# Dealing buffers, PSUM halves and two loads anew in the start of a two-layer conditioned convolution kernel

## The chip, the cores and the metric

The kernel runs on one core of a Trainium2 chip. TensorE multiplies into PSUM (eight banks, here two halves A and B of four banks each), VectorE (DVE) and ScalarE (ACT) read PSUM and SBUF, GpSimd (POOL) works in SBUF, and SyncE (SP) issues transfers. ScalarE issues a few transfers too; SP's and ScalarE's transfers go by two queues through the same 16 DMA engines. Everything is float32. The metric is device time in microseconds (us).

## The reference

128 samples `x[b]` of 128 channels by 2048 positions pass four residual layers, whose parameters depend on a vector `cond[b]` of 128 numbers:

```python
x = x + conv1d(x, w0, groups=4, taps=9, pad=4) + (cond @ c0.T)[:, :, None] + bias
x = x + einsum('boi,bih->boh', agg_w1, x) + agg_b1[:, :, None]
x = x + conv1d(x, w2, groups=4, taps=9, pad=4) + (cond @ c2.T)[:, :, None] + bias
x = x + einsum('boi,bih->boh', agg_w3, x) + agg_b3[:, :, None]
```

with, for layers 1 and 3, `att = softmax(mlp(cond))` over 8 experts, `agg_w = einsum('bk,koi->boi', att, weight)` (one 128 x 128 matrix for each sample) and `agg_b = att @ bias_k`.

## The kernel before, in words

**Two parts.** A start of some 65 us computes everything that depends on `cond` and is the same for all positions. Then a pipeline over 64 pairs of samples does the four layers. The trip of the pipeline for pair i is a step; steps 0 and 1 and the last four are written out, the others are a hardware loop.

**The start.** TensorE computes the attention and the bias table, then the *matrix sets*: for each of the two mixing layers the 128 matrices of 128 x 128 are computed in 8 sets of 2048 columns (16 sets in all, numbered j = 0 to 15, the first eight for the first mixing layer). A set is one `aggregate`: matmuls that fill one half of PSUM (L347), from `rows`, the experts' weights. It is then *evicted*, that is, copied from PSUM to a buffer in SBUF, its *home*: by ScalarE (`take_agg`, L576) or VectorE (L738, for the sets in `BY_DVE`). Then SP stores it to DRAM (`mix_dram`, `store_agg`, L227), 1 MB each. The homes are buffers that the pipeline uses later: `shared[0..1]` and `y[0..1]`. `AHEAD` = 14 sets are made before the first convolution, the last two between it and the first mix. Semaphores: `taken(j)` says that set j was evicted (TensorE may reuse the half), `agg_stored[j]` that its store has landed (its home may be reused). `half_of(j)` is the PSUM half and `home_of[j]` the home.

**Beside it.** SP loads the taps of the two convolutions (`load_taps(v)`, 0.75 MB each) and the inputs of the pairs (`load_x_on`, 2 MB a pair). GpSimd works the taps over (L289 to L294), first those of layer 0, then those of layer 2. VectorE makes four *differences* of a pair's inputs (BOTH, SIGNED, ONLY_EVEN, ONLY_ODD; `diff_of_xin`, L695), which the convolution's matmuls read instead of the inputs; four more of the first two layers' output (`diff_of_x2`) feed the second convolution.

**A convolution** (`conv`, L373) is 224 matmuls. ScalarE copies the sums out in six parts (`take_sums`, L603 to L616): three into `shared`, three into `y`. The third of five parts of the matmuls (ONLY_EVEN) waits for the first copy and for all four differences. VectorE then makes the two halves of the output in `y` (L748, L750). **A mix** (`mix`, L441) is 128 matmuls of `y` with the pair's matrices, which `load_mix_on` loads from `mix_dram` into `mixw` (L167, four transfers); ScalarE evicts it (L664, L625).

The order of step 0 on TensorE is: convolution of pair 0, sets 14 and 15, first mix of pair 0; then comes the convolution of pair 1, and then the second convolution of pair 0. Each engine works its instructions in the order written; the kernel has no scheduler. The waits that matter are these lines:

```python
        BY_DVE = (2, 4)
...
                if j >= len(homes):
                    act.wait_ge(agg_stored[same_home_before(j)], 16)
...
                    conv(0, 0, taken(AHEAD - 1), taken(AHEAD - 2), (1, 2, 4), nothing)
...
                    mix(0, 0, taken(AHEAD), taken(AHEAD), taken(AHEAD + 1), nothing)
```

The first two arguments of `conv` and `mix` after the numbers are the semaphores for the halves: the first convolution begins in half A.

## Time and profile before

| what | us |
|---|---|
| median of three runs (2497.75 to 2498.95) | 2497.8 |
| the profiled execution | 2493.67 |
| its span, from the first to the last instruction | 2491.9 |
| TensorE matmuls busy in it | 2460.8 (99%) |
| VectorE busy | 2136.1 (86%) |
| ScalarE busy | 1523.4 (61%) |
| GpSimd busy | 32.0 (1%) |

The times of the trace count from the start of the span of the profiled execution. A busy TensorE need not be TensorE at its peak. The DMA engines are busy 90% or more in the first fortieth of the span and about 40% in the others.

### The profile page before, as it was taken

Reading aid. Unit: us, or ns where it says so; the run is one execution under the profiler, and the core shown is the slowest. Engines: PE = TensorE matmul, PEld = TensorE weight load, DVE = VectorE, ACT = ScalarE, POOL = GpSimd, SP = SyncE. Lnnn points to the kernel's source line nnn. Section 1 sums busy time; section 2 is a strip of 40 time slices with the busy share of each in tenths; the row PEclk is TensorE's granted clock in tenths of the full one; section 3 lists DMA queues with packets and bytes.
Section 4 is the critical chain, followed back from the end, with each engine's and each line's share of the span. In section 5 each row is a group of like instructions: output and inputs, shape, how many; then the busy total and the mean of one; then the engine's idle time right before and its main releaser. Section 6 shows DMA issues by size and latency. Waiting matters only on the chain.

```text
span 2491.9 us, 99092 instructions
## 1 busy us (share of the span) xinstructions
PE 2460.8 (99%) x45256; PEld 1402.0 (56%) x45256; DVE 2136.1 (86%) x796; ACT 1523.4 (61%) x1116; POOL 32.0 (1%) x28
## 2 busy tenths in 40 slices
PE   7999999999999999999999999999999999999998
PEld 3444444444555555555666666666666666666664
DVE  6988988889889889889889888898898898898883
ACT  5566666666666666666666666666666666666665
POOL 5000000000000000000000000000000000000000
PEclk9999999999999999999999999999999999999999
DMA  9444444444444444444444454444444444444433
GB/s 361 149 145 150 126 132 159 130 126 157 138 126 145 149 126 137 152 132 126 150 145 126 137 157 128 127 159 135 126 150 144 126 142 150 129 128 154 139 95 120
DMA packets 186682, 357.23 MB, mean 143 GB/s; under 512 B 12754, under 2 KB 143834, under 8 KB 154010
## 3 DMA queue, kind: packets, MB, share of 16 engines
q1 hardware_dynamic: 184824, 352.50, 45.2%
q10 hardware_dynamic: 1826, 4.23, 0.5%
q8 instruction: 29, 0.48, 0.1%
q14 instruction: 3, 0.02, 0.0%
HBM read 205.69 MB, written 150.99 MB: 143 GB/s over the span
## 4 chain that ended last, share of the span: by engine, by line
PE 97%; DMA 1%; ACT 1%; DVE 1%; issue 0%; SPq 0%; ACTq 0%
PE psum L373 61%; PE psum L441 35%; DMA mix_dram<-y 1%; DMA out<-outb 0%; ACT y L576 0%; DVE h L730 0%; PE psum L300 0%; ACT outb L625 0%; DVE y L727 0%; PE psum L347 0%; DVE diff L695 0%; DVE shared L738 0%; DVE y L738 0%; DVE y L750 0%; ACT y L612 0%
## 5 line engine op out<-in xcount | busy, mean ns | idle before, releaser
L373 PE MATMUL psum<-diff,prod_w 32*64 32x512 f32 x28672 | 1684.0, 588 | 8.0 <-ACT y L576 2.5
L373 PEld LDWEIGHTS psum<-diff,prod_w 32*64 32x64 f32 x28672 | 908.1, 131 | 684.4 <-issue 401.9
L695 DVE TENSOR_TENSOR diff<-xin 128x2052 f32<-128x2052 f32 x256 | 994.0, 3929 | 288.4 <-PE psum L373 288.4
L441 PE MATMUL psum<-y,mixw 32*64 32x512 f32 x16384 | 1020.1, 588 | 5.5 <-ACT y L576 3.4
L441 PEld LDWEIGHTS psum<-y,mixw 32*64 32x64 f32 x16384 | 545.8, 131 | 371.2 <-issue 221.1
L695 DVE TENSOR_TENSOR diff<-x 128x2055 f32<-128x2055 f32 x256 | 571.2, 2299 | 4.7 <-ACT x L664 4.7
L625 ACT ACTIVATE outb<-psum,bias_now 128x2048 f32<-128x2048 f32 x129 | 252.2, 1956 | 197.9 <-PE psum L441 196.3
L664 ACT ACTIVATE x<-psum,bias_now 128x2048 f32<-128x2048 f32 x128 | 252.8, 1975 | 195.4 <-PE psum L441 195.4
L603 ACT COPY shared<-psum 128x2048 f32<-128x2048 f32 x128 | 239.1, 1868 | 170.4 <-PE psum L373 169.5
L748 DVE TENSOR_TENSOR y<-y,shared 128x2048 f32<-128x2048 f32 x128 | 293.1, 2290 | 38.2 <-ACT y L614 38.2
L616 ACT COPY y<-psum 128x2048 f32<-128x2048 f32 x128 | 239.2, 1869 | 93.6 <-PE psum L373 93.6
L750 DVE TENSOR_TENSOR y<-y,shared 128x2048 f32<-128x2048 f32 x128 | 293.3, 2291 | 1.6 <-ACT y L616 1.5
L612 ACT COPY y<-psum 128x1024 f32<-128x1024 f32 x128 | 129.6, 1012 | 190.1 <-PE psum L373 190.1
L606 ACT COPY shared<-psum 128x1024 f32<-128x1024 f32 x128 | 129.6, 1013 | 80.6 <-PE psum L373 80.6
L608 ACT COPY shared<-psum 128x1024 f32<-128x1024 f32 x128 | 129.6, 1012 | 1.1 <-PE psum L373 1.0
L614 ACT COPY y<-psum 128x1024 f32<-128x1024 f32 x128 | 129.6, 1013 | 0.7 <-PE psum L373 0.6
L637 ACT COPY bias_now<-bias_table 128x12 f32 (+1 forms) x66 | 13.3, 201 | 15.3 <-issue 7.8
L576 ACT COPY shared<-psum 128x2048 f32<-128x2048 f32 x7 | 12.9, 1869 | 9.5 <-PE psum L347 9.5
L576 ACT COPY y<-psum 128x2048 f32<-128x2048 f32 x7 | 12.9, 1874 | 6.1 <-DMA mix_dram<-y 3.6
L347 PE MATMUL psum<-outb,att_t 32*128 32x512 f32 x64 | 10.4, 741 | 4.4 <-ACT y L576 1.8
L347 PE MATMUL psum<-diff,att_t 32*128 32x512 f32 x64 | 8.3, 619 | 3.6 <-DVE y L738 1.6
L347 PEld LDWEIGHTS psum<-outb,att_t 32*128 32x128 f32 x64 | 2.9, 209 | 12.0 <-ACT shared L576 6.0
(61 smaller groups left out, 83.3 us busy)
## 6 DMA issues: line engine op xcount, KB each, us to landing
out<-outb SPq DMA_DIRECT2D x127, 1024.0 KB, 4.8
xin<-x SPq DMA_DIRECT2D x126, 1024.0 KB, 6.8
mixw<-mix_dram SPq DMA_DIRECT2D x508, 128.0 KB, 5.5
mix_dram<-shared SPq DMA_DIRECT2D x8, 1024.0 KB, 12.5
mix_dram<-y SPq DMA_DIRECT2D x8, 1024.0 KB, 12.0
xin<-x ACTq DMA_DIRECT2D x2, 1024.0 KB, 10.9
y<-experts ACTq DMA_DIRECT2D x2, 512.0 KB, 4.6
prod_w<-conv_w SPq DMA_DIRECT2D x4, 256.0 KB, 7.9
```

What stands on the lines that cost most here:

```text
L373: return pe.matmul(psum[cols, half, g, :], prod_w[v][at, kind, s, cols], moving, start=start, stop=stop, skip_group_check=True)
L441: mm = pe.matmul(psum[cols, half, r, :], mixw[home][at, b, g, cols], y[home][at, :, g, b, :], start=g == 0, stop=g == GROUPS - 1)
L603: nc.scalar.copy(shared[v][:, 0], psum[:, A, :, :]).then_inc(shared_ready[v], 1)
L606: nc.scalar.copy(shared[v][:, 1, 0:2], psum[:, B_HALF, 0:2, :]).then_inc(shared_ready[v], 1)
L608: nc.scalar.copy(shared[v][:, 1, 2:4], psum[:, B_HALF, 2:4, :]).then_inc(shared_ready[v], 1)
L612: nc.scalar.copy(into[:, 0, 0:2], psum[:, A, 0:2, :]).then_inc(sums_taken[v], 1)
L616: nc.scalar.copy(into[:, 1], psum[:, B_HALF, :, :]).then_inc(sums_taken[v], 1)
L625: nc.scalar.activation(outb[:, b, :].rearrange("p (m j r) -> p m j r", j=PAR, r=PH)[:, at], psum[:, b, :, :].rearrange("p r (j m) -> p m j ...
L664: nc.scalar.activation(into, psum[:, b, :, :].rearrange("p r (j m) -> p j r m", j=PAR), ACT.Identity, bias=bias_now[:, 2 * PB + b, 0:1]).t ...
L695: nc.vector.tensor_tensor(into(kind), in0, in1, op).then_inc(diff_ready[v], 1)
L748: nc.vector.tensor_tensor(flat[:, 0], flat[:, 0], kept[:, 1], ALU.subtract).then_inc(y_ready[v], 1)
L750: nc.vector.tensor_tensor(flat[:, 1], flat[:, 1], kept[:, 0], ALU.add).then_inc(y_ready[v], 1)
```

## The change

It is confined to the start and to step 0.

- **Evictions.** VectorE evicts sets 3 and 5 (the fourth and the sixth) instead of 2 and 4. Set 2 goes to half A, and from there even sets go to A and odd ones to B; the first convolution starts in A behind set 12, and needs set 13's half later.
- **Homes.** There are ten instead of eight: both halves of `rows[0]` (which is `diff2`, free once the first eight sets are made) come in. Sets 14 and 15 go there and no longer to `y[1]`. VectorE's first `diff_of_x2`, which writes `diff2`, waits for their stores.
- **Loads.** The taps of layer 2 are loaded behind the first eight stores instead of before all. The inputs of pair 1 are issued by SP behind store 8, waiting there for the four differences of pair 0, instead of by ScalarE.
- **ScalarE.** The loads of pair 0's matrices (`first_matrices`) are issued behind the third copy of the first convolution instead of before the first. The first copy waits for store 6, the second for store 7, where the first waited for stores 8 and 9.
- **GpSimd.** Its work on the taps of layer 2 waits for the four differences of pair 0.

```diff
-        homes = [shared[0][:, 0], shared[0][:, 1], shared[1][:, 0], shared[1][:, 1],
-                 staging[:, 0], staging[:, 1], early[:, 0:2].rearrange("p n c -> p (n c)"),
-                 early[:, 2:4].rearrange("p n c -> p (n c)")]
+        homes = [shared[1][:, 0], shared[1][:, 1], early[:, 0:2].rearrange("p n c -> p (n c)"),
+                 early[:, 2:4].rearrange("p n c -> p (n c)"), staging[:, 0], staging[:, 1],
+                 shared[0][:, 0], shared[0][:, 1], rows[0][:, 0:PH * BANK], rows[0][:, PH * BANK:]]
...
-        home_of = [j % len(homes) for j in range(AHEAD)] + [4, 5]
-        LAST_IN_SHARED, LAST_IN_Y = ((8, 9), (10, 11)), ((6, 7), (14, 15))
+        home_of = list(range(len(homes))) + [0, 1, 4, 5, 8, 9]
+        LAST_IN_SHARED, LAST_IN_Y, LAST_IN_DIFF = ((6, 7), (10, 11)), ((2, 3), (12, 13)), (14, 15)
...
-            return A if j < 2 else 1 - j % 2 if j < AHEAD else j % 2
-
-        BY_DVE = (2, 4)
+            return A if j == 1 else j % 2
+
+        BY_DVE = (3, 5)
...
             load_rows(1)
-            load_taps(1)
...
-            for j in range(AHEAD):
+            for j in range(SETS):
                 store_agg(j)
+            load_taps(1)
+            store_agg(SETS)
+            sp.wait_ge(diff_ready[0], PRODUCTS)
+            load_x_on(sp, 1)
+            for j in range(SETS + 1, AHEAD):
+                store_agg(j)
...
+                if v == 1:
+                    pool.wait_ge(diff_ready[0], PRODUCTS)
...
+            pe.wait_ge(*taken(1))
+            aggregate(0, 2, half_of(2))
             pe.wait_ge(bias_ready, 2)
-            aggregate(0, 2, half_of(2))
-            for j in range(3, AHEAD):
+            aggregate(0, 3, half_of(3))
+            for j in range(4, AHEAD):
...
-                    conv(0, 0, taken(AHEAD - 1), taken(AHEAD - 2), (1, 2, 4), nothing)
+                    conv(0, 0, taken(AHEAD - 2), taken(AHEAD - 1), (1, 2, 4), nothing)
...
-                if j == AHEAD - 1:
-                    act.wait_ge(diff_ready[0], PRODUCTS)
-                    load_x_on(act, 1)
-
-            act.wait_ge(taps_ready, 1)
-            for j in range(SETS):
-                act.wait_ge(agg_stored[j], 16)
-            load_mix_on(act, 0, 0)
+
+            def first_matrices():
+                act.wait_ge(taps_ready, 1)
+                for j in range(SETS):
+                    act.wait_ge(agg_stored[j], 16)
+                load_mix_on(act, 0, 0)
...
-                    all_stored(LAST_IN_SHARED[v])
+                    act.wait_ge(agg_stored[LAST_IN_SHARED[v][0]], 16)
...
+                if whole(n) and n == 0:
+                    act.wait_ge(agg_stored[LAST_IN_SHARED[v][1]], 16)
...
+                behind_signed()
                 if whole(n) and n == 0:
-                    all_stored(LAST_IN_Y[v])
+                    for j in LAST_IN_Y[v]:
+                        act.wait_ge(agg_stored[j], 16)
...
+                if whole(i) and i == 0:
+                    take_sums(0, 0, behind_signed=first_matrices)
...
+                if whole(n) and n == 0:
+                    for j in LAST_IN_DIFF:
+                        dve.wait_ge(agg_stored[j], 16)
```

What this does to the order on ScalarE and on SP is seen best in the rows themselves. First ScalarE, from its tenth eviction of a set to the last copy of the first convolution, before the change (buffers by number; `mixw0` are the matrices of the first mixing layer, and a wait on `agg_stored9` is for the landing of set 9's store):

```order
L576 COPY y1<-psum 128x2048 [waits agg_stored4,agg_pe]
L576 COPY y1<-psum 128x2048 [waits agg_stored5,agg_pe]
L161 DMA xin<-x 128x2048 [waits diff_ready0]
L161 DMA xin<-x 128x2048
L167 DMA mixw0<-mix_dram0 32x8x128 [waits agg_stored4,agg_stored3,agg_stored5,agg_stored2,agg_stored6,agg_stored1,agg_stored7,agg_stored0,taps_ready]
L167 DMA mixw0<-mix_dram0 32x8x128 x3
L637 COPY bias_now<-bias_table 128x12 [waits bias_ready]
L603 COPY shared0<-psum 128x2048 [waits agg_stored9,conv_done0,agg_stored8,picked]
L606 COPY shared0<-psum 128x1024 [waits conv_done0]
L608 COPY shared0<-psum 128x1024 [waits conv_done0]
L612 COPY y0<-psum 128x1024 [waits conv_done0,agg_stored7,agg_stored6]
```

The same stretch on ScalarE after the change:

```order
L586 COPY y1<-psum 128x2048 [waits agg_stored4,agg_pe]
L586 COPY y1<-psum 128x2048 [waits agg_stored5,agg_pe]
L648 COPY bias_now<-bias_table 128x12 [waits bias_ready]
L610 COPY shared0<-psum 128x2048 [waits conv_done0,agg_stored6,picked]
L615 COPY shared0<-psum 128x1024 [waits conv_done0,agg_stored7]
L617 COPY shared0<-psum 128x1024 [waits conv_done0]
L167 DMA mixw0<-mix_dram0 32x8x128 [waits agg_stored4,agg_stored3,agg_stored5,agg_stored2,agg_stored6,agg_stored1,agg_stored7,agg_stored0,taps_ready]
L167 DMA mixw0<-mix_dram0 32x8x128 x3
L623 COPY y0<-psum 128x1024 [waits conv_done0,agg_stored3,agg_stored2]
L625 COPY y0<-psum 128x1024 [waits conv_done0]
L627 COPY y0<-psum 128x2048 [waits conv_done0]
L586 COPY diff2<-psum 128x2048 [waits agg_stored8,agg_pe]
```

The two issues of inputs are gone from ScalarE, the four issues of matrices stand between the third and the fourth copy, and set 14 (the last row) goes to `diff2` behind the store of set 8.

On SP, the stores and what stands between them, one piece of the difference (`xin` are the inputs, `prod_w` and `mixw` receive the taps of layer 2):

```order
+L226 DMA mix_dram<-shared 512x1x512 [waits agg_taken_act] x2
 L205 DMA prod_w<-conv_w 128x512
 L205 DMA mixw<-conv_w 128x512
 L205 DMA prod_w<-conv_w 128x512
...
+L226 DMA mix_dram<-diff 512x1x512 [waits agg_taken_act]
+L161 DMA xin<-x 128x2048 [waits diff_ready0]
+L161 DMA xin<-x 128x2048
+L226 DMA mix_dram<-diff 512x1x512 [waits agg_taken_act]
+L226 DMA mix_dram<-shared 512x1x512 [waits agg_taken_act] x2
+L226 DMA mix_dram<-y 512x1x512 [waits agg_taken_act] x2
+L226 DMA mix_dram<-diff 512x1x512 [waits agg_taken_act] x2
```

The taps now stand behind the stores of sets 6 and 7, and the wait for the differences with the inputs of pair 1 between the stores of sets 8 and 9.

## Rows read from the trace of the kernel before

**Rows 1.** Groups of lines by form, 100 to 2400 us: name, count | busy us, mean ns | idle before

```profile
L373 PE MATMUL psum<-diff,prod_w 32*64 32x512 f32 x27186 | 1595.0, 587 | 1.0 <-issue 1.0
L441 PE MATMUL psum<-y,mixw 32*64 32x512 f32 x15616 | 970.8, 587 | 0.0
```

**Rows 2.** Chain that ended last, start of the program: start us, us, what

```profile
19.49 1.19 PE psum L347 x8
...
26.57 10.00 DMA mix_dram<-y
...
44.41 19.84 DMA mix_dram<-y
...
64.33 1.88 ACT y L576
...
66.34 9.07 PE psum L441 x122
```

**Rows 3.** Timeline of ScalarE and its queue: start us, us, what [idle before]

```profile
21.55 1.86 ACT L576 COPY shared<-psum 128x2048 f32<-128x2048 f32 x1 [3.81 <-PE psum L347]
...
27.80 3.63 ACT L576 COPY y<-psum 128x2048 f32<-128x2048 f32 x2 [0.83 <-PE psum L347]
...
46.32 4.05 ACTq L167 DMA_DIRECT2D mixw<-mix_dram  x4
...
51.49 1.87 ACT L603 COPY shared<-psum 128x2048 f32<-128x2048 f32 x1 [0.88 <-DMA mix_dram<-shared]
...
57.28 1.01 ACT L612 COPY y<-psum 128x1024 f32<-128x1024 f32 x1 [1.56 <-PE psum L373]
58.19 1.02 ACT L614 COPY y<-psum 128x1024 f32<-128x1024 f32 x1
...
95.53 1.01 ACT L608 COPY shared<-psum 128x1024 f32<-128x1024 f32 x1
```

**Rows 4.** Timeline of VectorE, 26 to 90 us

```profile
26.46 17.90 DVE L695 TENSOR_TENSOR diff<-xin 128x2052 f32<-128x2052 f32 x4
...
61.73 2.29 DVE L750 TENSOR_TENSOR y<-y,shared 128x2048 f32<-128x2048 f32 x1
63.94 15.35 DVE L695 TENSOR_TENSOR diff<-xin 128x2052 f32<-128x2052 f32 x4
79.22 8.91 DVE L695 TENSOR_TENSOR diff<-x 128x2055 f32<-128x2055 f32 x4
```

**Rows 5.** Timeline of TensorE, 42 to 100 us

```profile
42.73 8.53 PE L373 MATMUL psum<-diff,prod_w 32*64 32x512 f32 x120 [2.49 <-ACT y L576]
53.50 6.27 PE L373 MATMUL psum<-diff,prod_w 32*64 32x512 f32 x104 [2.23 <-ACT shared L603]
...
87.44 12.29 PE L373 MATMUL psum<-diff,prod_w 32*64 32x512 f32 x224 [0.41 <-ACT y L614]
```

**Rows 6.** Windows: engines' busy us (x), granted clock, DMA share, GB/s

```profile
26.00:44.00 18.00, 11.43 (x80) 3.63 (x84) 18.00 (x5) 15.38 (x9) 14.43 (x4) 0.86 1.05 409
42.70:45.70 3.00, 2.96 (x32) 1.50 (x36) 1.66 (x1) 0.00 (x0) 0.00 (x0) 0.51 1.06 410
66.20:69.50 3.30, 3.16 (x32) 1.50 (x36) 3.30 (x2) 1.87 (x1) 0.00 (x0) 0.50 0.66 245
```

**Rows 7.** Line L167 on ScalarE's queue, 46 to 50 us, issues and landings

```profile
L167 ACTq DMA_DIRECT2D mixw<-mix_dram x4: 576/912/1558, 46.3 to 49.8; - x4
...
DMA to landing us min/median/max: 12.8/13.3/15.6
```

**Rows 8.** Line L161 on ScalarE's queue, 44.3 to 45.5 us

```profile
L161 ACTq DMA_DIRECT2D xin<-x x2: 333/775/1217, 44.4 to 44.8; - x2
...
DMA to landing us min/median/max: 9.3/10.9/12.5
```

**Rows 9.** DMA queues, 57.5 to 62.5 us (q1: SP, q10: ScalarE): packets, MB, share

```profile
q1 hardware_dynamic: 787, 1.57, 81.1%
q10 hardware_dynamic: 777, 0.37, 25.4%
```

More of the change, by code:

```diff
@@ L580, in _, with nothing, take_sums @@
                     take_agg(j)
-                if j == AHEAD - 1:
-                    act.wait_ge(diff_ready[0], PRODUCTS)
-                    load_x_on(act, 1)
-            act.wait_ge(taps_ready, 1)
-            for j in range(SETS):
-                act.wait_ge(agg_stored[j], 16)
-            load_mix_on(act, 0, 0)
-            def all_stored(sets):
-                for j in sets:
+            def first_matrices():
+                act.wait_ge(taps_ready, 1)
+                for j in range(SETS):
                     act.wait_ge(agg_stored[j], 16)
-            def take_sums(v, n, halves=(A, B_HALF), home=None):
+                load_mix_on(act, 0, 0)
+            def nothing():
+                pass
+            def take_sums(v, n, halves=(A, B_HALF), home=None, behind_signed=nothing):
                 A, B_HALF = halves
@@ L638, in step @@
                 act.wait_ge(picked, i + 1)
-                if has_front(i):
+                if whole(i) and i == 0:
+                    take_sums(0, 0, behind_signed=first_matrices)
+                elif has_front(i):
                     take_sums(0, i)
```

## The prediction

> **What bounds the kernel now.** I read the groups of lines between 100 and 2400 us first: convolutions and mixes keep TensorE busy back to back, with 1.0 us of idle time before all of them [rows 1]. Nothing in the loop is touched by the change but waits that come true once, so the loop's length stays and the question is only when it starts. I therefore read the chain before 90 us [rows 2]. The reader should see that it is not TensorE there: it runs through the landings of two stores into `mix_dram` (those of sets 4 and 12) and an eviction on ScalarE (L576), and arrives at the first mix at 66.34 us. So the number that matters is the start of the first mix, and every microsecond gained there should be a microsecond of the whole.
>
> What holds that start? The eviction of set 14 begins at 64.33 and ends at 66.2, because its buffer (y1) is also that of set 12, whose store lands at 44.41 + 19.84 = 64.25 [rows 2]. The outputs of the first convolution were ready at 61.73 + 2.29 = 64.0 [rows 4], and the mix's weights landed at 49.8 + 15.6 = 65.4 [rows 7]. So three things come within 2.2 us of one another, and moving one alone would give little. The change moves all three.
>
> **DMA is the background.** From 26 to 44 us it moves 409 GB/s without a gap [rows 6]: a store of 1 MB takes 2.56 us, a pair of inputs (2 MB) 5.1, a set of taps (0.75 MB) 1.9. The order in SP's queue thus decides landing times. Before, set 4 lands at 36.57 [rows 2], and set 8, four stores on, at 46.8. After, the second layer's taps stand behind set 7, so sets 0 to 7 land 1.9 us earlier: set 4 at 34.7, set 6 at 39.8, set 7 at 42.3; then the taps at 44.3, set 8 at 46.8, the inputs of pair 1 at about 52, set 9 at 54.5, and one more each 2.56 us. The issue of those inputs waits for four differences on VectorE (below, about 42.5), behind it on SP stand sets 9 to 15; as the queue holds work until 46.8, this wait costs nothing unless the differences come after that.
>
> **Step 1, evictions.** Before, set 2 waits for the bias (begins 19.49), and while VectorE has sets 2 and 4, ScalarE stands idle again and again, 3.81 us before the first of its copies and 0.83 before the one from which it runs on [rows 3]. After, set 2 goes into half A behind the eviction of set 1 and needs no bias; the bias chain ends at 19.1, so it starts 0.3 us earlier. I rolled the chain forward with the rows' durations: 1.19 for the matmuls of one set, 1.86 for a ScalarE copy, 2.29 for a VectorE pass over 2048 columns [rows 2 to 4]. Set 2 evicted by 22.2, set 3 (VectorE) by 23.5, set 4 by 25.3, set 5 (VectorE) by 27.0, set 6 from 26.5, and from there ScalarE copies without a gap, eight in 14.7 us, to 41.2 (before from 27.80 until just ahead of 42.73). The home changes keep it gapless: sets 10 to 13 wait for stores 0, 1, 4, 5, landed by 37.3 when they are wanted at 33.9 to 39.3. The first convolution, which waited for set 13 (42.73) [rows 5], now waits for set 12: 39.4. **3.3 us earlier.** Set 13's half is wanted three microseconds later.
>
> **Step 2, the first convolution.** Before, it ran in two pieces: 8.53 us, 2.23 us waiting for ScalarE's first copy (late at 51.49, behind the issues of the inputs and the weights and the landing of set 9), then the rest [rows 3, 5]. The granted clock was 0.51 for its first 3.0 us [rows 6], after TensorE had waited 2.49 us [rows 5]; those 3.0 us at the lower level (1.2 GHz) did the work of 1.5. After, ScalarE has nothing before its first copy but store 6 (39.8), and TensorE works some 1.2 of each 1.86 us until 38.7, so I take the upper level. In the undisturbed convolution the third copy (L608) ends at 95.53 + 1.01, 9.1 us after the start at 87.44 [rows 3, 5]; 0.4 of that goes to eight matmuls of another stage, which the first has not, at 12.29 us for 224 matmuls. So it ends at 48.1.
>
> **Step 3, the weight loads.** They stand now behind this third copy. Four issues took ScalarE 4.05 us [rows 3], against a gap of 1.56 us there. So the copies that follow (0.91 from one to the next, 1.02 the second) run from 52.2 to 54.1, and the last one until 56.0; VectorE's two outputs take 2.29 each and end at 58.7. The eviction of set 14 ends at 57.8; its buffer is free (set 8, 46.8). Set 15 waits for set 9, 54.5, and is wanted at 57.8. What ends last is then the weights: issued from 48.1. In the trace before, the inputs issued at 44.4 on ScalarE's queue land by 44.8 + 12.5 = 57.3 [rows 8], which at half the rate for 2.1 MB (10.3 us) means a pick-up 2.6 us after the issue; the weights, behind them, need from 57.3 to 65.4, 8.1 us, while the stores share. After: 50.7 at the earliest for the pick-up, about 52 when the inputs on SP's queue are through, and 8.1 more: 58.8 to 60.3. The bound from the other side is the measured 15.6 us of such a load [rows 7]: 48.1 + 15.6 = 63.7. I take 60.4, near the first, since the inputs that made up most of the 15.6 are no longer ahead in the same queue.
>
> **Sum.** First mix at 60.4 for 66.34: **5.9 us**. The mix itself began at clock 0.50 for 3.3 us [rows 6]; a gap in TensorE's work stands before it again, so this stays, give or take 1.7. Behind it nothing is late: VectorE starts the differences of pair 1 at 58.7 (before 63.94) and needs 15.35 and then 8.91 us as before [rows 4]. Its new wait, sets 14 and 15, is met at about 71.5 where it is wanted at 74.0. GpSimd's second tap stage, which was busy 14.43 us beside the differences [rows 6], begins at about 45 and would end by 60 at that length, where it is wanted at 81. The profiled execution took 2493.67 us around its span of 2491.9; the median of the runs shown is 2497.8, 4.1 above it, and the stretch that changes has no part in this that I can see. So 2497.8 - 5.9 = **2491.9**.
>
> **The rivals.** 0.2% is 5.0 us, about what a measurement of this kernel can tell from no change.
>
> (a) *The weights land before the outputs are ready.* If the four issues are quick (0.58 us each, as the last two were) and the pick-up is at 50.7, the mix starts at about 58: gain 8, 2489.8. The 8.1 us of sharing speaks against it. Chance 0.11.
>
> (b) *The weights wait for the inputs on the other queue.* While stores and weights share the engines the two queues' packets are equal in number, 787 to 777, though they move 1.57 and 0.37 MB [rows 9]: an engine takes turns by packet. A small packet then waits for a large one, and if the inputs already taken up have to go first, up to 5.1 us are added to the pick-up: mix at 62 to 64.5, gain 2 to 4.5, say 3.2, and 2494.6. For it: the pick-up of 2.6 us itself shows work standing ahead. Against: only 1.3 us of the inputs are left at 50.7. Chance 0.22. The Trainium skill (DMA: Bandwidth & Descriptors, Queues, rings and completion order) says that an engine goes round-robin between the queues but drains a whole packet of typically 9 to 17 descriptors from one before it switches. By that rule the inputs taken up on an engine would go as a turn or two before the weights get theirs, which is this rival; equal numbers agree with turns, but nothing here shows their length.
>
> (c) *The clock.* If the longer idle time before the mix leaves it at 0.50 for twice as long, or if the convolution starts at 0.50 as before, 1.7 us are lost: gain 4.2, 2493.6. Chance 0.08.
>
> (d) *Slower.* VectorE's new wait: differences of the second layer stand behind stores 14 and 15, and behind them on VectorE the outputs of pair 1. The second convolution starts at 81.5 and wants its first difference (2.3 us), so the stores cost nothing until 79.2, eat the gain by 85, and make the kernel slower by over 0.2% from 90: 18 us behind the queue's account. That would need SP to stand at the inputs' wait past 60 us, or DMA at 70% of its rate. With the last store at 92 us the whole is 12.8 - 5.9 = 6.9 longer: 2504.7. Chance 0.04.
>
> (e) *The change does not do what it says*: the DMA backlog is only passed on, to set 15 or the loads of the next pairs, and returns as stalls between 75 and 110 us. Total DMA work is unchanged. Gain 0 to 2, 2496.8. Chance 0.08.
>
> **The numbers.** Forecast 0.45. Faster by over 0.2%: the forecast without its lower tail (0.40), (a), and 0.05 of (b) and (c): 0.56. Slower: (d) and 0.02 left for what I don't see: 0.06. The rest, 0.38, within. The range goes from (a), with the mix at the upper clock (2489.0), to the middle of (e) (2496.8); it leaves out (d) and part of (e). The forecast's own range is 2490.7 to 2493.
>
> **What would show it.** In the profile after: the first matmul of the first convolution near 39.4 at full clock and no gap inside it; ScalarE's four issues between its third and fourth copy, near 48; VectorE's four differences in 15.5 us and not 17.9, if it was GpSimd beside them that drew them out; the first mix near 60.4, released by the weights. Wrong would be: the mix released by anything else later than 61, a wait on VectorE before its first difference of the second layer, or a convolution that starts at the lower clock.

## The result and the profile after

The changed kernel takes **2487.5 us** (median of 13 runs, 2485.9 to 2491.6), the kernel before beside it 2495.3 (13 runs, 2491.8 to 2499.0): ratio 0.9969, 95% interval 0.9962 to 0.9977, that is 7.7 us less (5.7 to 9.5). Two repetitions gave 0.9972 (0.9962 to 0.9982) and 0.9975 (0.9966 to 0.9984). It is faster by more than 0.2%, as forecast, but 2487.5 lies below the forecast range of 2489.0 to 2496.8. The profiled execution took 2488.0 us around a span of 2486.2; the one before had a span of 2491.9.

TensorE in the profile after (timeline; start us, us, what, idle before and its releaser), which answers to [rows 5]:

```profile
41.24 13.01 PE L383 MATMUL psum<-diff,prod_w 32*64 32x512 f32 x224 [0.72 <-ACT y L586]
54.18 1.14 PE L355 MATMUL psum<-outb,att_t 32*128 32x512 f32 x8
56.23 1.14 PE L355 MATMUL psum<-outb,att_t 32*128 32x512 f32 x8 [0.91 <-ACT y L627]
61.86 10.50 PE L451 MATMUL psum<-y,mixw 32*64 32x512 f32 x124 [4.49 <-DMA mixw<-mix_dram]
...
84.57 12.29 PE L383 MATMUL psum<-diff,prod_w 32*64 32x512 f32 x224 [0.37 <-ACT y L625]
```

The first convolution is one piece of 224 matmuls, where [rows 5] have 120, a wait of 2.23 us, and 104. The gap ahead of it is 0.72 us instead of 2.49. What releases the first mix is the landing of the weights, and it stands at 61.86 instead of 66.34. The next row tells where that comes from, ScalarE and its queue:

```profile
39.16 3.71 ACT L586 COPY y<-psum 128x2048 f32<-128x2048 f32 x2
...
45.97 1.86 ACT L610 COPY shared<-psum 128x2048 f32<-128x2048 f32 x1 [3.01 <-PE psum L383]
...
49.37 1.02 ACT L617 COPY shared<-psum 128x1024 f32<-128x1024 f32 x1
49.64 2.37 ACTq L167 DMA_DIRECT2D mixw<-mix_dram  x4
52.14 1.01 ACT L623 COPY y<-psum 128x1024 f32<-128x1024 f32 x1 [1.75 <-PE psum L383]
...
58.67 1.87 ACT L586 COPY diff<-psum 128x2048 f32<-128x2048 f32 x1 [0.72 <-DMA mix_dram<-diff]
```

The first copy of the convolution waits for TensorE alone (51.49 before, 45.97 now), the four issues are over in 2.37 us (4.05 before), and set 15 is evicted by 60.5, ahead of the mix. The weights' issues and landings, which answer to [rows 7]:

```profile
L167 ACTq DMA_DIRECT2D mixw<-mix_dram x4: 343/585/774, 49.6 to 51.2; - x4
DMA to landing us min/median/max: 7.0/8.8/10.5
```

VectorE, which answers to [rows 4]:

```profile
28.98 15.30 DVE L711 TENSOR_TENSOR diff<-xin 128x2052 f32<-128x2052 f32 x4
...
56.37 2.28 DVE L766 TENSOR_TENSOR y<-y,shared 128x2048 f32<-128x2048 f32 x1
58.58 15.28 DVE L711 TENSOR_TENSOR diff<-xin 128x2052 f32<-128x2052 f32 x4
74.93 8.93 DVE L711 TENSOR_TENSOR diff<-x 128x2055 f32<-128x2055 f32 x4 [1.07 <-ACT x L677]
```

The last row is the first work behind the new wait for stores 14 and 15: in this trace it was released by ScalarE, so the wait cost nothing here (in two later traces a store released it; see the rivals below). Windows of the profile after (busy us, count in brackets, then granted clock, DMA share, GB/s):

```profile
9.90:13.30 3.40, 3.40 (x20) 1.38 (x12) 0.59 (x3) 0.00 (x0) 0.13 (x1) 0.50 1.01 336
14.00:61.00 47.00, 34.53 (x368) 14.44 (x366) 33.30 (x15) 33.03 (x21) 14.34 (x15) 1.00 1.00 370
61.10:67.90 6.80, 6.04 (x58) 3.02 (x65) 6.80 (x3) 0.00 (x0) 0.00 (x0) 0.50 1.05 409
```

The convolution ran at clock 1.00 (2.4 GHz), the mix at 0.50 (1.2 GHz) for 6.8 us, twice the length in [rows 6]. The first window lies in code that both kernels share, and in the first trace of the kernel before it had clock 1.00. So the two traces do not compare like with like, and the experiments begin there.

### The profile page after: what moved, and what is told of

Same layout as the page of the kernel before. It is cut to its first block, busy times and chain, and to the rows that moved or that the text cites. A ratio compares the mean times of both kernels' runs of the same rounds, so it can differ in the third digit from the quotient of the medians.

```text
span 2486.2 us, 99095 instructions
## 1 busy us (share of the span) xinstructions
PE 2459.6 (99%) x45256; PEld 1549.1 (62%) x45256; DVE 2133.8 (86%) x796; ACT 1522.9 (61%) x1116; POOL 22.5 (1%) x28
## 4 chain that ended last, share of the span: by engine, by line
PE 97%; ACT 1%; DMA 1%; DVE 0%; issue 0%; ACTq 0%
PE psum L383 62%; PE psum L451 35%; DMA mixw<-mix_dram 0%; ACT shared L586 0%; ACT y L586 0%; DMA out<-outb 0%; DVE h L746 0%; PE psum L308 0%; PE psum L355 0%; PE psum L339 0%; ACT outb L636 0%; ACT diff L586 0%; DVE y L743 0%; DVE diff L711 0%; DVE y L766 0%
## 5 line engine op out<-in xcount | busy, mean ns | idle before, releaser
L383 PEld LDWEIGHTS psum<-diff,prod_w 32*64 32x64 f32 x28672 | 1007.3, 131 | 583.3 <-issue 218.6
L451 PE MATMUL psum<-y,mixw 32*64 32x512 f32 x16384 | 1031.7, 589 | 6.5 <-DMA mixw<-mix_dram 4.5
L451 PEld LDWEIGHTS psum<-y,mixw 32*64 32x64 f32 x16384 | 607.0, 132 | 319.9 <-issue 138.8
L627 ACT COPY y<-psum 128x2048 f32<-128x2048 f32 x128 | 239.4, 1871 | 93.2 <-PE psum L383 93.2
L648 ACT COPY bias_now<-bias_table 128x12 f32 (+1 forms) x66 | 13.3, 202 | 7.5
L586 ACT COPY y<-psum 128x2048 f32<-128x2048 f32 x4 | 7.4, 1904 | 3.6 <-PE psum L355 3.6
```

The source lines that it names most:

```text
L383: return pe.matmul(psum[cols, half, g, :], prod_w[v][at, kind, s, cols], moving, start=start, stop=stop, skip_group_check=True)
L451: mm = pe.matmul(psum[cols, half, r, :], mixw[home][at, b, g, cols], y[home][at, :, g, b, :], start=g == 0, stop=g == GROUPS - 1)
L627: nc.scalar.copy(into[:, 1], psum[:, B_HALF, :, :]).then_inc(sums_taken[v], 1)
```

## The experiments

**The same kernels again.** What of 2491.9 against 2486.2 is the change, and what the execution?

> The changed kernel once more, beside the next three on one chip. Theory (TensorE's first matmuls run at clock 0.50 between 9.9 and 13.3 us in some executions and not in others, and this alone is 2.4 us): its trace either repeats the first convolution at 41.2 or shows it at 38.9; the loop takes the same time to 0.1 us; the ratio to the kernel before is again 0.9962 to 0.9977. Rival (the first result was a favourable draw): ratio above 0.9977.

> The kernel before once more, unchanged, against itself, for its own spread and a second trace of it. Theory one (the gain beyond 5.9 us is chance: a stretch at the lower clock near the kernel's end and a stall at the loop's exit that come in some executions of any kernel): ratio 1.000 within its interval, and this trace may lack the stretch at clock .50 at 2459 us that the first trace had; its ScalarE reaches its 17th pair eviction at 236.5 us give or take 1 from the span's start (before's first trace: 236.46), 5 to 7 us behind the second trace of the changed kernel (about 231.3). Theory two (before loses time at its tail or exit because of its buffers): the stretch at .50 in the tail stands in this trace too, and the time from the 17th pair eviction to the end is 1.7 us or more over that of the changed kernel again.

> The changed kernel a third time, on the same chip as the run of the kernel before, unchanged. Theory one: ratio 0.996 to 0.998, and the 17th pair eviction at 231 us if the first conv runs at clock 1.0 from the start, at 233.6 us if a stretch at .50 lies at about 10 to 13 us (2.4 us, as in its first trace). Theory two gives the same ratio, and no trace of the changed kernel has a stretch at .50 behind 2440 us but for the last 3 us.

Measured, changed kernel: 2487.1 us (2485.9 to 2489.2) and 2487.3 (2486.0 to 2490.0). Kernel before: 2495.3 (2492.5 to 2496.7) against its own 2493.8 in 21 runs, ratio 1.0003 (0.9993 to 1.0012). Times in the five traces, in us from the span's start:

| trace | clock 9.9 to 13.3 | conv starts | mix starts | its first eviction | rest of the span | 0.50 in the tail |
|---|---|---|---|---|---|---|
| before | 1.00 | 42.73 | 66.34 | 72.62 | 2419.3 | yes |
| before, again | 0.57 | 45.29 | 69.07 | 76.83 | 2418.1 | yes |
| changed | 0.50 | 41.24 | 61.86 | 69.55 | 2416.7 | no |
| changed, second | 1.00 | 38.83 | 59.71 | 67.26 | 2417.0 | no |
| changed, third | 1.00 | 38.90 | 59.45 | 65.56 | 2419.2 | yes |

("Rest" is the span less the column ahead of it.) A stretch at 0.50 at the program's begin costs 2.3 to 2.6 us in either kernel, 42.73 to 45.29 and 38.90 to 41.24. The rest of the span differs by up to 2.6 us, between traces with and without a stretch at 0.50 near the end. Neither stretch belongs to one kernel. The third trace of the changed kernel has its stretch there too, as the windows of the kernel before, of its repetition and of that trace show:

```profile
2458.90:2462.30 3.40, 3.40 (x40) 1.52 (x32) 3.40 (x3) 1.97 (x1) 0.00 (x0) 0.50 0.04 14
```

```profile
2461.20:2464.50 3.30, 3.30 (x40) 1.43 (x34) 3.30 (x2) 1.52 (x1) 0.00 (x0) 0.50 0.00 0
```

```profile
2451.70:2455.00 3.30, 3.30 (x40) 1.51 (x32) 3.30 (x2) 1.97 (x1) 0.00 (x0) 0.50 0.00 0
```

So theory two (a tail that is the old kernel's) falls. Of theory one the main part holds, that both stretches come in either kernel; its landmark, the 17th pair eviction, came at 240.67 us in the second trace of before and at 229.59 in the third of the changed kernel, where it had 236.5 and 231, so executions differ by more than it allowed. Like with like are the first trace of before and the third of the changed kernel, both with the fast begin (clock 1.00 from 9.9 to 13.3 us) and the stretch at 0.50 in the tail. Their spans are 2491.9 and 2484.8, 7.1 us apart, of which 6.9 stand at the start of the first mix (66.34 less 59.45) and 7.1 at its first eviction. The pair with the slow begin gives 7.2 and 7.3 (69.07 less 61.86, 76.83 less 69.55). TensorE in the third trace, and its windows:

```profile
38.90 13.01 PE L383 MATMUL psum<-diff,prod_w 32*64 32x512 f32 x224 [0.72 <-ACT y L586]
...
59.45 8.91 PE L451 MATMUL psum<-y,mixw 32*64 32x512 f32 x124 [4.41 <-DMA mixw<-mix_dram]
```

```profile
14.00:58.00 44.00, 32.34 (x358) 13.62 (x356) 30.36 (x14) 31.84 (x21) 14.45 (x15) 1.00 1.03 388
59.00:62.30 3.30, 2.85 (x29) 1.50 (x36) 3.30 (x2) 0.00 (x0) 0.00 (x0) 0.50 1.05 409
```

Here the mix has 3.3 us at 0.50 behind an idle time of 4.41 us; in the second trace the clock was at 0.50 for 6.8 us (58.7 to 65.5) around an idle time of 4.75 us, and the mix took 10.36 instead of 8.91.

**The clock in all executions.** A trace shows one execution, but each timed run lists its mean granted clock (to 0.001; the mean over many runs is finer):

| kernel | runs | mean time | mean clock |
|---|---|---|---|
| before | 31 | 2493.9 | 0.9962 |
| changed (the two repetitions) | 20 | 2487.5 | 0.9977 |
| evictions alone | 11 | 2493.2 | 0.9967 |
| all but the evictions | 11 | 2495.2 | 0.9957 |
| wait for set 13 / the same, filled | 11 / 11 | 2491.7 / 2491.6 | 0.9970 / 0.9969 |
| before, filled | 11 | 2495.8 | 0.9969 |
| gap ahead of the mix filled | 11 | 2487.7 | 0.9981 |
| weights early / weights on SP | 10 / 11 | 2486.2 / 2487.3 | 0.9980 / 0.9980 |
| inputs on ScalarE | 11 | 2488.4 | 0.9974 |
| taps first, GpSimd beside / inputs first | 11 / 11 | 2489.2 / 2491.8 | 0.9971 / 0.9975 |

A clock 0.0015 lower over 2490 us is half speed for 7.5 us, a loss of at most 3.7 us, reached if TensorE always had work then. Among runs of one kernel, 0.001 of clock went with 1.2 us (48 and 44 runs of before at 0.996 and 0.997: 2494.2 and 2493.0) to 1.9 us (9 and 24 of the changed at 0.997 and 0.998: 2488.9 and 2487.0). By that relation 1.8 to 2.9 of the 6.4 us between the means would belong to the clock, and the rest, 3.5 to 4.6, to shorter waits. This is an estimate from numbers that move together, and no run sets the clock by itself; the five runs of before at 0.998 were no faster (2493.2).

**One half of the change each.** The evictions alone, on the kernel before (VectorE takes sets 3 and 5, set 2 ahead of the bias, halves dealt anew):

```diff
-            return A if j < 2 else 1 - j % 2 if j < AHEAD else j % 2
-
-        BY_DVE = (2, 4)
+            return A if j == 1 else j % 2
+
+        BY_DVE = (3, 5)
...
```

> The kernel before with the eviction part of the change alone: VectorE evicts sets 3 and 5, set 2 goes to half A ahead of the wait for the bias, the first convolution starts behind set 12. Homes, loads and their places as before. Theory (the DMA chain and ScalarE's place in it hold the start): the convolution begins near 39 to 40 instead of 42.73, but its first copy stays at 51.5, behind store 9, so the mix stays at 66 to 66.5 and the time is that of the kernel before within 0.5 us, but for the clock. Rival (the evictions are the path): mix and time 2 to 3 us earlier.

Measured: 2492.5 us, ratio 0.9994 (0.9985 to 1.0003). TensorE and ScalarE:

```profile
38.86 7.10 PE L375 MATMUL psum<-diff,prod_w 32*64 32x512 f32 x120 [0.72 <-ACT y L578]
57.07 8.75 PE L375 MATMUL psum<-diff,prod_w 32*64 32x512 f32 x104 [11.11 <-ACT shared L605]
70.14 7.53 PE L443 MATMUL psum<-y,mixw 32*64 32x512 f32 x124 [1.19 <-DVE y L752]
```

```profile
55.06 1.86 ACT L605 COPY shared<-psum 128x2048 f32<-128x2048 f32 x1 [5.52 <-DMA mix_dram<-shared]
```

The convolution starts 3.9 us earlier, as in the whole change, and then stands for 11.11 us: its first copy waits for the store of set 9, whose home is `shared[0]`. In this trace the mix is 3.8 us later than before. And all but the evictions, the inverse of that diff on the changed kernel:

> The changed kernel without the eviction part: VectorE evicts sets 2 and 4, the old halves, the bias wait ahead of set 2, the first convolution behind set 13; homes, loads and places as changed. Theory: with the clock at 1.0 all through, the convolution starts 3.3 us later than in the changed kernel (42.2 for 38.9), the copies, the issue of the weights and the mix move with it by 2.5 to 3.3 us; the time lies 2.5 to 3.3 us above the changed kernel's and 4 to 5 below that of before. Rival (DMA alone sets the weights' landing): within 1 us of the changed kernel.

Measured: 2495.4 us, 1.0003 (0.9994 to 1.0012), in a trace with the slow begin:

```profile
44.16 16.02 PE L381 MATMUL psum<-diff,prod_w 32*64 32x512 f32 x224 [2.49 <-ACT y L584]
...
67.96 8.89 PE L449 MATMUL psum<-y,mixw 32*64 32x512 f32 x124 [4.18 <-DMA mixw<-mix_dram]
```

The gap of 2.49 us is back and the convolution takes 16.02 us (clock 0.50 until 50.2). The weights go out behind its third copy, at 55.58, and hold the mix. A time 4 to 5 us below that of before had been expected. **Neither half gives a gain that can be measured; both together give 6.5 to 7.7 us.** That is shown by the medians. The two traces show which waits there are and not their usual size, since each is of the slowest execution of its eleven (2496.9 and 2499.2 us). In the clock table the evictions alone have a third of the change's clock (0.9967), and the rest alone has less than before (0.9957).

**How much is the clock?** The changed kernel with a wait for set 13 ahead of the convolution again, that wait filled with 7 small matmuls, and the kernel before filled likewise:

```diff
+                    pe.wait_ge(*taken(AHEAD - 2))
+                    for _ in range(7):
+                        pe.matmul(psum[:, A, 0, 0:B], eye_sb, eye_sb, start=True, stop=True)
+                    pe.wait_ge(*taken(AHEAD - 1))
                     conv(0, 0, taken(AHEAD - 2), taken(AHEAD - 1), (1, 2, 4), nothing)
```

> The changed kernel with one wait added: the first convolution starts when set 13 is evicted, as before, and not set 12. TensorE's gap ahead of it grows from 0.7 to 2.6 us. Theory (the gap brings the convolution to the lower clock, which is what costs most in the old order): it starts 1.85 us later and then runs at 0.50 for 3.4 to 6.8 us; its end, the weights and the mix come 3.5 to 5.2 us later; the time is 3.5 to 5 us above the changed kernel's. Rival (only the wait counts): 1.9 us or less.

> The same, with seven matmuls of 128 x 128 without use in that gap, behind the eviction of set 12; they write a bank that the convolution overwrites. Theory: the clock stays at 1.0, the convolution starts 1.85 us later than in the changed kernel and runs 13.0 us; the time is 1.5 to 2 us above the changed kernel's and 2 to 3 us below the run without them. Rival: no better than without them.

> The kernel before with the same seven matmuls between the evictions of sets 12 and 13. Theory: the first convolution keeps the clock and reaches its wait 1.7 us earlier, but there it still waits for ScalarE's first copy, which stands behind the issues and the store of set 9 (51.5); so the start is as before within 0.5 us, and if anything the longer wait drops the clock there. Rival (the clock alone is what the change gave back): 1.7 us or more faster than before.

Measured: 2491.8 us, 0.9992 (0.9983 to 1.0001); 2491.3, 0.9992 (0.9983 to 1.0001); 2495.0, 1.0007 (0.9998 to 1.0016). The wait alone takes 4.7 of the 7 us back. Its trace has the slow begin, as the profile after has:

```profile
43.37 14.71 PE L383 MATMUL psum<-diff,prod_w 32*64 32x512 f32 x224 [2.40 <-ACT y L587]
...
66.20 10.43 PE L451 MATMUL psum<-y,mixw 32*64 32x512 f32 x124 [4.95 <-DMA mixw<-mix_dram]
```

The convolution starts 2.1 us later (43.37 for 41.24) and takes 1.7 longer, and the mix starts 4.3 later. With the filler it takes 13.02 us and the mix starts at 62.92. But over 11 executions the filler left the mean clock where it was (0.9970 and 0.9969), and the time too, so its one trace does not stand for the others. In the kernel before it raises the clock (0.9962 to 0.9969) and the time does not fall. Its trace shows why: the convolution at full clock only stands longer for ScalarE's late copy (3.37 us for 2.23), and behind that wait the clock falls, so that the second piece takes 9.15 us where [rows 5] have 6.27:

```profile
52.61 9.15 PE L373 MATMUL psum<-diff,prod_w 32*64 32x512 f32 x104 [3.37 <-ACT shared L606]
```

```profile
52.60:59.30 6.70, 6.69 (x72) 2.52 (x80) 0.00 (x0) 1.80 (x3) 0.00 (x0) 0.56 1.03 389
```

Filling the gap ahead of the mix in the changed kernel (14 small matmuls behind set 14's eviction):

> The changed kernel with 14 matmuls of 128 x 128 without use put between set 15 and the first mix, once half A is free; they write a bank that the mix overwrites. Theory (the time lost behind the start is the granted clock, 0.50 for 6.8 us after the gap before the mix): TensorE works from 58.0 to 61.3, the mix runs at clock 1.0 from its start, conv of pair 1 begins 3.4 us earlier, and the time falls by 1.7 to 3.4 us; the runs also scatter less. Rival (the clock has another cause than the gap): the mix is at 0.50 as before, same time, or up to 1 us more if the fillers delay it.

Measured: 2487.5, 0.9977 (0.9968 to 0.9986).

```profile
60.90 7.51 PE L452 MATMUL psum<-y,mixw 32*64 32x512 f32 x124 [1.88 <-issue]
```

7.51 us instead of 8.91 to 10.50, the highest mean clock of all (0.9981), and nothing of it in the median. In this trace the last of the weights landed at 60.8 (issued at 48.9, 11.9 us to landing), so the mix ends at 68.4, where that of the third trace, which starts at 59.45 and takes 8.91, ends too. Against the second trace, whose mix ends at 70.1, it gains 1.7 us. Why the weights landed later here, and whether they do in other executions, is not shown.

**The weights.** Back ahead of the first copy (the diff is the inverse of `behind_signed=first_matrices`); on SP, ahead of the inputs, with ScalarE's issues taken out (the diff shows SP's part); and the inputs of pair 1 on ScalarE's queue again, ahead of the weights:

```diff
             store_agg(SETS)
+            sp.wait_ge(taps_ready, 1)
+            for j in range(SETS):
+                sp.wait_ge(agg_stored[j], 16)
+            load_mix_on(sp, 0, 0)
             sp.wait_ge(diff_ready[0], PRODUCTS)
             load_x_on(sp, 1)
```

> The changed kernel with the four loads of pair 0's matrices put back ahead of ScalarE's first copy; all else stays. Theory (the weights release the first mix, at 61.86 in the changed kernel): they wait only for store 7 (43.5) and are issued ahead of the inputs of pair 1, so they land by about 52; the first copy stays near 46; the mix is then released by the outputs or by set 14 near 58 to 58.7, some 3.4 us earlier, and the time falls by 3 to 4 us, to about 2484. Rival (the issues ahead of the first copy hold the convolution, which is why they had been moved): the first copy moves to 48 or later, a gap of 2 us opens in the convolution, and the time is that of the changed kernel or 1 to 2 us more.

> The changed kernel with the four loads of pair 0's matrices issued by SP, behind store 8 and the landings of stores 0 to 7, ahead of the inputs of pair 1; ScalarE issues none. Theory: the weights land by 51, ScalarE's fourth copy follows its third at once, the mix starts near 58, the time is 3.5 to 4.5 us below the changed kernel's. Rival (the inputs or set 9's store become late instead, since all of SP's queue moves back by the weights): the mix starts after 60 or VectorE waits for the inputs at 58.6, gain below 2 us.

> The changed kernel with the inputs of pair 1 issued by ScalarE again, after its last eviction and the four differences, as in the kernel before; the loads of the matrices stay behind the third copy. Theory: the inputs share the engines with stores 9 to 11 packet by packet, land later (near 57), and the weights, in the same queue behind them, land at 64 or later; the first mix starts near 64 to 65, 2 to 3 us later than in the changed kernel. Rival (which queue they stand in does not matter, DMA is one pool): mix within 0.5 us of 61.9.

Measured: 2486.6 (0.9970, 0.9960 to 0.9979), 2486.9 (0.9972, 0.9963 to 0.9981) and 2488.3 (0.9978, 0.9969 to 0.9987). The 3 to 4.5 us less that were expected of the first two did not come. The first mix in the three traces:

```profile
60.51 9.21 PE L451 MATMUL psum<-y,mixw 32*64 32x512 f32 x124 [2.19 <-DMA mixw<-mix_dram]
```

```profile
57.16 3.66 PE L455 MATMUL psum<-y,mixw 32*64 32x512 f32 x56 [2.18 <-DVE y L768]
61.45 3.69 PE L455 MATMUL psum<-y,mixw 32*64 32x512 f32 x64 [0.63 <-ACT diff L590]
...
73.53 5.41 PE L387 MATMUL psum<-diff,prod_w 32*64 32x512 f32 x96 [1.52 <-DVE diff L713]
```

```profile
60.71 9.94 PE L449 MATMUL psum<-y,mixw 32*64 32x512 f32 x124 [5.67 <-DMA mixw<-mix_dram]
```

Issued early on ScalarE's queue, from 43.6 to 46.0, the weights still release the mix, 1.35 us earlier than in the profile after (both traces have the slow begin). The last of the four needed 14.4 us to land. The queues of that run from 48 to 54 us, while SP's held the inputs, and those of the third trace from 52 to 56, while it held stores, show why (packets, MB, share):

```profile
q1 hardware_dynamic: 327, 2.06, 93.0%
q10 hardware_dynamic: 328, 0.16, 10.2%
```

```profile
q1 hardware_dynamic: 626, 1.25, 80.4%
q10 hardware_dynamic: 629, 0.30, 25.7%
```

The two queues move packet for packet both times. Beside the large packets of the inputs the weights get 55 packets a microsecond, beside the stores 157: from one queue to the other, what stands beside a load sets its rate. On SP's queue, with ScalarE's queue empty, the four land in 3.7 to 6.7 us each and hold nothing. The mix then starts 2.3 us earlier than in the best trace of the changed kernel, and no microsecond of it reaches the median. The trace says where it goes: the second half of the mix waits for set 15 (0.63), the next convolution for VectorE's differences of pair 1 (1.52), and so does a later one (1.31). VectorE is 1.4 us later here than in the third trace (74.88 for 73.47): its differences of pair 1 took 16.45 us for 15.33, with GpSimd's work beside their start, and it waits for the last store for 1.41 us (1.13 in the third trace):

```profile
74.88 8.93 DVE L713 TENSOR_TENSOR diff<-x 128x2055 f32<-128x2055 f32 x4 [1.41 <-DMA mix_dram<-diff]
...
99.80 0.66 PE L387 MATMUL psum<-diff,prod_w 32*64 32x512 f32 x4 [1.31 <-DVE diff L713]
```

The queue of the inputs is worth 1.0 to 1.3 us of mix start (60.71 against 59.45 and 59.71), and 1 us in the median lies within the intervals.

**GpSimd beside VectorE, and inputs first.** In the first, the taps are loaded ahead of the stores again and GpSimd's wait is out. In the second, SP loads inputs and weights of the mix ahead of the store of set 8, and VectorE makes one difference of pair 1 before the outputs:

```diff
-                if v == 1:
-                    pool.wait_ge(diff_ready[0], PRODUCTS)
```

> The changed kernel with the taps of layer 2 loaded ahead of all stores again and GpSimd not waiting for the four differences. Theory (these two parts hide nothing and cost nothing, since the queue holds work until 46.8 in either order): VectorE's four differences take 17.9 us again for 15.3, the inputs are issued 2.5 us later, their landing moves by under 1 us, the mix by under 0.5 us, the time by under 0.5 us. Rival (they carry part of the gain): 1 to 2.5 us above the changed kernel.

> A version that goes beyond the change. SP's queue behind store 7: inputs of pair 1, weights (issued by SP), stores 8 and 9, the taps of layer 2, stores 10 to 13; GpSimd's second tap stage waits for eight differences; VectorE makes pair 1's first difference before the outputs of pair 0's first convolution. Theory (behind an earlier mix, VectorE's four differences of pair 1, 15.4 us from the outputs, and the store of set 9 are what ends last): inputs land near 49, the first difference is done by 53 and the other three by 69.5 instead of 73.5; the mix starts near 58 and has no gap at its second half; the time falls 3 to 4 us below the changed kernel's. Rival (the difference delays the outputs by as much as it gains, or GpSimd beside VectorE draws its work out): within 1 us of it.

Measured: 2489.4 (0.9979, 0.9970 to 0.9988) and 2491.3 (0.9987, 0.9978 to 0.9996). In the first, VectorE's differences take 17.59 us (15.30 in the profile after), with GpSimd beside them; the convolution starts at 38.95 all the same, but the mix only at 60.82, 1.1 to 1.4 us later than in the two traces of the changed kernel that begin like it, where under 0.5 had been expected. Its mean time lies 1.7 us above that of the changed kernel and its mean clock, 0.9971, below. So these two parts seem to carry part of the gain, which is the rival of that expectation; the intervals do not settle it. In the second, the stores come back as a wait on VectorE:

```profile
79.28 10.12 DVE L714 TENSOR_TENSOR diff<-x 128x2055 f32<-128x2055 f32 x4 [6.38 <-DMA mix_dram<-diff]
```

```profile
105.40 0.66 PE L388 MATMUL psum<-diff,prod_w 32*64 32x512 f32 x4 [3.36 <-DVE diff L714]
```

That is the mechanism of rival (d), at a place where it reaches TensorE: the second row is TensorE waiting 3.36 us for a difference. The version is slower than the changed kernel by 4 us, where 3 to 4 us less had been expected.

## Why the number missed and the mechanism held

**The step that failed is the base of the sum.** The prediction noted that the profiled execution took 2493.67 us and the median of the three runs 2497.8, said that the stretch that changes has no part in those 4.1 us, and wrote "So 2497.8 - 5.9 = 2491.9". The three runs (2497.75 to 2498.95) lay at the upper end of the kernel's spread: in later runs its medians were 2493.7 to 2495.3, and single runs went down to 2490.5. Of the 4.4 us by which 2491.9 missed, 2.5 are this base (2497.8 for 2495.3 beside the changed kernel) and 1.9 the size of the gain (5.9 for the 7.8 between these two medians). With 2495.3 the same sum gives 2489.4, and the whole range, moved by 2.5, takes in 2487.5. From the profiled execution's own time, 2493.67 - 5.9 gives 2487.8, close to the measured 2487.5, but that is in part luck: the base of that sum is lower than the medians, and the gain is too small, and the two nearly cancel. The range took in bounds for every term of the change and none for the base. The table above has what such a base is made of: 2.3 to 2.6 us at the begin, up to 2.6 in the rest.

**The size** of 5.9 us lies in the interval (5.7 to 9.5), near its lower end; in like traces it is 7.1. The terms, against the third trace of the changed kernel, which begins like that of before:

- *Step 1.* Convolution at 39.4; measured 38.90. The gain is 3.8 us for 3.3. The step has ScalarE copy "without a gap, eight in 14.7 us". That is about what the eight took before (27.80 to 42.59), and there they had a gap of 0.38 us, in a stretch where the clock was 0.86 [rows 6]:

```profile
35.42 3.63 ACT L576 COPY shared<-psum 128x2048 f32<-128x2048 f32 x2 [0.38 <-PE psum L347]
```

In the third trace, at 1.00 from 14 to 58 us, the eight have no gap and take 14.3 (26.27 to 40.53). That the clock made the gap is likely; no run isolates it.
- *Step 2.* One piece at the upper clock: 13.01 us, as forecast. The third copy ends at 47.03 + 1.02 = 48.05 in that trace, forecast 48.1, because two errors cancel: the start is 0.5 us early, and from the start it is 9.15 us, not 8.7, so the 0.4 taken off for eight matmuls was not there.
- *Step 3.* Mix at 60.4, released by the weights; measured 59.45, and by the weights in all three traces. From issue to mix it is 12.2 to 12.5 us in all three traces (49.64 to 61.86, 47.23 to 59.71, 47.30 to 59.45), where the forecast has 12.3. What was 0.8 us wrong is the start: the step issues the weights when the third copy ends (48.1), and ScalarE issues the first at 47.30, while that copy (47.03 to 48.05) still runs. The pick-up of 2.6 us rests on a wrong reading, that the inputs got "half the rate": the packets are equal in number, but from 50 to 56 us of the trace of before ScalarE's queue moved 1.85 MB of 2.39, and its first packet came no earlier than 48.5, over 4 us behind the issue. It did no harm, since the sum took 52 as the start of the sharing; in the third trace the first packets move between 50.5 and 51. And "four issues take 4.05 us" was wrong without harm: 2.37 us, hidden but for 0.2 of the copy behind them (a gap of 1.75 for 1.56).
- *The mix at 0.50 for 3.3 us*: 3.3 once, 6.8 twice (and 6.7 in the second trace of before). Half of rival (c), that the mix stays at 0.50 for twice as long, came true in two of three traces.
- *The clock as a whole* was in the sum with 1.5 us (3.0 us at the lower level that fall out of the convolution); over all executions it is 1.8 to 2.9, by the relation above.
- *Differences in 15.5 us, no wait on VectorE, GpSimd hidden*: 15.30 and hidden. The wait, which the prediction names as a sign of being wrong, is there in two of the three traces (rival (d) below). The run with GpSimd beside them gave 17.59, so GpSimd is what drew them out.
- *"Every microsecond gained at the first mix should be a microsecond of the whole."* True here (6.9 of 7.1), but only this far: the run with weights on SP gained 2.3 us more at the mix and nothing in the time, as set 15 and VectorE's differences of pair 1 were next.

**Rivals.** (a) is out: in the changed kernel the weights never landed first, and the run in which they do (on SP's queue) starts the mix at 57.16 and gains nothing that can be measured. (b), weights waiting for the inputs on the other queue, is right in that large packets slow the small ones (the last load took 14.4 us with the inputs beside it), but was priced at 62 to 64.5 and did not come, as the inputs were nearly through when the weights' first packets moved. From 50 to 58 us of the third trace the two queues moved 1209 packets with 2.55 MB and 1054 packets with 0.51 MB. The Trainium skill (DMA: Bandwidth & Descriptors, Queues, rings and completion order) has the engines go round-robin by packet; the near-equal counts agree, here and in the 327 beside 328 above, and the long turns by which I had raised that price did not show as time. (e) did not come. (d) came without its price: in the second and the third trace VectorE's first difference of the second layer is released by a store of `diff2`.

```profile
72.75 8.93 DVE L711 TENSOR_TENSOR diff<-x 128x2055 f32<-128x2055 f32 x4 [0.94 <-DMA mix_dram<-diff]
```

```profile
73.47 8.93 DVE L711 TENSOR_TENSOR diff<-x 128x2055 f32<-128x2055 f32 x4 [1.13 <-DMA mix_dram<-diff]
```

VectorE's differences of pair 1 had ended at 72.33 in the third trace, so the stores were 1.1 us late. TensorE did not feel it: its second convolution starts behind ScalarE's copy, with a gap of 0.37 or 0.38 us, in all three traces.

**What stays open.** The stretch at the begin stood in 7 of the 16 traces, too few to say that it is as frequent in both kernels. Where the executions without a trace had their slow stretches is unknown, and with it why the filled wait keeps the mean clock of the plain one. That a mix 1.4 to 3 us shorter (filled gap) leaves the median where it was is explained for its one trace only, by weights that landed later. Which of the two parts, taps or GpSimd, costs the 1.7 us of the run with both taken back is open.

## What to carry to other kernels

Give the base of a sum a spread of its own, and do not add a gain read from the rows of one execution to the median of a few others: here three runs sat 2.5 to 4.1 us over what more runs gave, about half of the whole effect. Compare two profiles only where their stretches at half clock lie alike, or take a second trace of each. When several chains arrive within 2 us of one another, expect that one half of a change gives nothing, and price the halves together. Count the gaps on TensorE ahead of the loop, since each may bring a stretch at half clock, and read the mean clock of all runs, not of the profiled one alone. An engine that starts earlier only moves the stall to whatever its consumer's buffer waits for (11.11 us behind the store of set 9, in one trace), so follow the homes of buffers before moving an eviction. Where two queues are busy, put a small load that is wanted soon on the queue of the large ones, ahead of them: here that took it from 14.4 us to under 7.

## What the runs showed of the hardware

- The same instructions ran at clock 0.50 or 1.00 between 9.9 and 13.3 us from one execution to the next, in both kernels, and it cost 2.3 to 2.6 us. The Trainium skill (TensorE: Matmul & The Clock Gate, Part 1) says that the chip's watch over TensorE's activity is free-running and does not reset when a kernel starts; traces that differ with the same program agree with that.
- An idle time of 4.41 us on TensorE came with 3.3 us at 0.50, one of 4.49 with 6.8 us, one of 4.75 with 6.8 us; in the trace of before, one of 2.49 us with 3.0 us at 0.51. In one trace, 28 matmul instructions of 128x128 in that gap (two for each of the 14) went with a clock of 1.00 and a mix of 7.51 us.
- VectorE's four differences took 15.30 us alone and 17.59 with GpSimd's work beside them.
- A load of 0.5 MB on ScalarE's queue needed 12.2 to 12.5 us from its first issue while SP's queue held 2 MB of inputs and the stores, at 384 to 396 GB/s in all from 50 to 58 us. Its four parts landed in 3.7 to 6.7 us each when they stood in SP's queue ahead of the inputs.
- With both queues busy, packets went one for one whatever their size: 327 of 2.06 MB beside 328 of 0.16 MB in 6 us, 626 of 1.25 MB beside 629 of 0.30 MB in 4 us.
- ScalarE issued a transfer while its copy was running (issue at 47.30, copy from 47.03 to 48.05). Four issues took 2.33 to 2.41 us in the three traces of the changed kernel and 4.05 us in the first of before.
